# Layer 1 attention on one core: the value products of two steps issued in one block, with four slots for the exponentials

## What is computed

```python
q = jnp.dot(x, Wq).reshape(b, t, H, HD).transpose(0, 2, 1, 3)
kv = jnp.dot(x, Wkv).reshape(b, t, G, 2, HD).transpose(2, 3, 0, 1, 4)
k, v = (kv[:, 0], kv[:, 1])          # each repeated for the 4 heads of its group
scores = jnp.einsum('bhqd,bhkd->bhqk', q, k)
scores = jnp.where(causal[None, None], -jnp.inf, scores)
weights = jax.nn.softmax(scores * (1.0 / HD ** 0.5), axis=-1)
ctx = jnp.einsum('bhqk,bhkd->bhqd', weights, v)
```

## Time and profile before

| | |
|---|---|
| three runs | 1753.5, 1756.12, 1759.4 us; median 1756.12 |
| profiled execution | 1757.35 us, of which the span of the trace is 1755.6 us |
| PE busy over the span | 1650.3 us (94%) |
| DVE, ACT, POOL busy | 1085.6 (62%), 847.8 (48%), 709.1 (40%) |
| stage of layer 1 attention | about 1290 to 1560 us |

### The profile page before, as it was taken

How to read it: one execution, slowest core, us unless ns; L and a number is a source line. 1 busy time by engine, 2 the same in 40 slices (tenths; PEclk the granted TensorE clock), 3 DMA queues, 4 the chain that set the end, 5 groups by cost and what they waited for, 6 DMA issues and landing times. The chain is left out here.

```text
span 1755.6 us, 27326 instructions
## 1 busy us (share of the span) xinstructions
PE 1650.3 (94%) x8874; PEld 1232.9 (70%) x8874; DVE 1085.6 (62%) x2491; ACT 847.8 (48%) x1595; POOL 709.1 (40%) x735
## 2 busy tenths in 40 slices
PE   5899999999988999999999999799999999999998
PEld 5688887788777667766677766577765555568887
DVE  3545657999838677777777776345756777510222
ACT  3456556443326555555555555343135565653321
POOL 1112213444647566665566665385001111322221
PEclk9999999999999999999999999899969999999999
DMA  8522223221110001000001000463622342231111
GB/s 238 167 76 91 88 73 102 56 65 29 54 37 1 19 19 37 19 19 19 19 19 37 19 19 13 127 197 121 174 34 50 73 76 62 51 95 61 48 49 48
DMA packets 110716, 114.16 MB, mean 65 GB/s; under 512 B 39520, under 2 KB 71744, under 8 KB 110592
## 3 DMA queue, kind: packets, MB, share of 16 engines
q1 hardware_dynamic: 108288, 108.40, 22.2%
q10 hardware_dynamic: 2304, 4.20, 0.7%
HBM read 83.97 MB, written 28.44 MB: 64 GB/s over the span
## 5 line engine op out<-in xcount | busy, mean ns | idle before, releaser
L1447 ACT ACTIVATE a_p<-a_sm,a_nmax 128x640 f32<-128x640 f32 (+7 forms) x256 | 198.7, 778 | 142.9 <-DVE a_nmax L1408 141.3
L1490 POOL TENSOR_SCALAR a_p<-a_p,a_rinv 128x640 f32<-128x640 f32 (+7 forms) x256 | 190.6, 748 | 167.8 <-DVE a_rinv L1416 166.4
L1408 DVE CUSTOM_DVE_ANT_0 a_sm<-ps,maskb 128x640 f32<-128x640 f32 (+7 forms) x256 | 192.0, 750 | 100.4 <-PE ps L1352 98.4
L2334 DVE CUSTOM_DVE_ANT_0 ga_sm<-ps,strip 128x640 f32<-128x640 f32 (+1 forms) x224 | 163.3, 755 | 80.4 <-PE ps L2241 78.8
L2354 ACT ACTIVATE ga_pt<-ps 128x1024 f32<-128x1024 f32 (+1 forms) x192 | 148.1, 810 | 114.3 <-PE ps L2264 113.5
L1364 PE MATMUL ps<-ident,a_p 128*128 128x128 f32 x1152 | 172.5, 275 | 12.8 <-DVE a_pt L1423 12.5
L1364 PEld LDWEIGHTS ps<-ident,a_p 128*128 128x128 f32 x1152 | 132.8, 140 | 39.5 <-issue 16.9
L2394 POOL TENSOR_SCALAR_AFFINE_SELECT ga_pt<-ga_pt 128x512 f32<-128x512 f32 x64 | 40.6, 635 | 287.5 <-ACT ga_pt L2354 287.3
L1352 PE MATMUL ps<-kh,lq_qh 128*128 128x512 f32 (+3 forms) x384 | 129.0, 390 | 17.5 <-DVE a_nmax L1408 10.6
L923 DVE SCALAR_TENSOR_TENSOR idx<-ix_r,ix_sgc,idx 128x256 f32<-128x256 f32 (+6 forms) x105 | 90.8, 885 | 76.2 <-ACT ix_r L888 76.2
L1379 PE MATMUL ps<-a_pt,vst 128*64 128x512 f32 (+3 forms) x768 | 135.7, 496 | 1.8 <-DVE a_pt L1423 1.1
(11 more groups left out here) (319 smaller groups left out, 4015.2 us busy)
## 6 DMA issues: line engine op xcount, KB each, us to landing
ctx_d<-a_ctxst SPq DMA_DIRECT2D x16, 512.0 KB, 2.9
idx<-ctx_d SPq DMA_DIRECT2D x32, 256.0 KB, 3.7
idx<-wvo_d SPq DMA_DIRECT2D x32, 256.0 KB, 4.4
ga_qst<-qkd SPq DMA_DIRECT2D x42, 128.0 KB, 4.2
f_wr<-in_L_ffn_w SPq DMA_DIRECT2D x18, 256.0 KB, 2.7
x<-in_L_attn_hidden_states SPq DMA_DIRECT2D x16, 256.0 KB, 4.5
op_wo<-in_L_attn_o_w SPq DMA_DIRECT2D x8, 512.0 KB, 4.4
ix_w<-in_L_attn_idx_wq_w SPq DMA_DIRECT2D x64, 64.0 KB, 1.9
```

Of the source, the lines that this page charges most:

```text
L1408: dve.tensor_tensor_reduce(out=sm[kind][:, 0:w], in0=slots[kind][:, 0:w], in1=maskb[:, MASK_OFF[t]:MASK_OFF[t + 1]], scale=-scale, scalar= ...
L1447: act.activation(p[kind][:, v // 2 % 2, 0:w], sm[kind][:, 0:w], ACT.Exp, bias=nmax[:, v % 4:v % 4 + 1], scale=-1.0, accum_out=rsum[:, v % ...
L1490: pool.tensor_scalar(mine, mine, rinv[:, v % 4:v % 4 + 1], 1.0, ALU.mult, ALU.mult).then_inc(norm_done, 1)
L2334: dve.tensor_tensor_reduce(out=sm[kind][:, 0:w], in0=slots[kind][:, 0:w], in1=strip[:, S - w:], scale=-1.0, scalar=3.0e38, op0=ALU.add, op ...
```

## The change

Two edits in `grouped_attention`. The ring `ga_pt` has four slots, not three, so that ACT's exponential of step n waits for the weigh of step n - 4. And PE issues no `weigh` in even steps; in an odd step (from the third of the whole stage on) it issues two at the place of the one, that of three steps before and that of two steps before.

```diff
-    RING = 3
+    RING = 4
     NB = NB1
     LAG = 2
     LEAD = 3
...
                         if s == NSTEP - LEAD and g + 1 < G1:
                             turn(g + 1)
-                        if g * NSTEP + s >= LAG:
-                            weigh((g * NSTEP + s - LAG) // NSTEP, (g * NSTEP + s - LAG) % NSTEP)
+                        if s % 2 and g * NSTEP + s > LAG:
+                            for n in (g * NSTEP + s - LAG - 1, g * NSTEP + s - LAG):
+                                weigh(n // NSTEP, n % NSTEP)
                         for v in units[two:]:
                             score(later, v)
```

## The result

The change makes the kernel slower. The median of six runs is 1795.6 us (1787.5 to 1796.9) against 1757.8 of before (1753.5 to 1765.3); the ratio is 1.021, 95% interval 1.019 to 1.024. The forecast was 1772, range 1754 to 1782: the direction is right, the size is not: 38 us came where 16 were forecast.

The account below looks back on a forecast made before the run. PE's list (94% busy) and the chain unit, DVE maximum, next unit in the same slot were taken as bounds. Terms 11.3 + 1.5 + 2.2 + 1.0 = 16.0 us gave 1773.4, or 1772 by the median; range 1754 to 1782.

Parts of the forecast that it names:

- the walk: Layer 1's attention, one full group followed by pairs of steps: lateness sums to 2.27 us per group, 16.0 in all; 70%.
- 0, 1: Step 0's weigh was free beside a DVE wait; step 1 takes two weighs, 0.79 us for 0.37: +0.42.
- 2, 3: Step 2 loses a 512 weigh (-1.18) but waits 0.53 for its slot; step 3 gets 0.85 more: +0.20.
- 4, 5: Step 4's 640 waits for the 1024; step 5's block grows by 0.43, partly hidden by its DVE wait: +0.1.
- 6, 7: Largest term: step 6's 512 weigh lay inside a wait; its stream returns in step 7 and DVE falls behind: +0.85.
- 8, 9: Step 8 waits 0.77 for the 896's slot, so some 0.4 is gained; step 9 gets 0.85 more: +0.5.
- 10, 11: Keys p=1 of step 11 wait 0.52 us for ACT's exponentials, against 0.32 saved: +0.2.
- pauses over 1 us in steps 0, 6 and 8: Sign expected on PE before the unit weight loads (L2241), PE's DVE waits rising from some 3 to some 7 us per group.
- Groups 0, 6 and 7: Groups outside the five full ones: 1.5 us for group 0's later steps, 2.2 for group 6, 1.0 for group 7.
- The rival's own price: Clock falls to 0.50 with longer PE pauses: ten us in each of seven groups, 35 us, 1792; 3%.
- The gain side: Joining two weighs saves up to 0.08 + 0.14 + 0.10 = 0.32 us per block in switches and fixed cost.
- The prediction's sum over all 47 blocks: Rival that PE alone counts: 47 switches saved at 0.32 us in all eight groups, 15.0 us, 1742; 15%.

Follow-up runs that it names:

- The fill run: Changed kernel with keys p=1 of even steps in groups 0 to 6 issued twice and 128-column units seven times: 1780.5 us, ratio 1.012 against before.
- the short maximum: DVE's maximum over only the first 128 keys per unit: 1731.6 us in the order of before, 1724.0 changed, 1730.0 with only wide steps' weighs joined.

## Why the prediction was right and wrong

**The waits (the path right, the size somewhat too small).** At full clock one can add the pairs of steps of the changed kernel from keys to keys: steps 0 and 1 from 1450.45 to 1457.09, 6.64 us; 2 and 3, 4.07; 4 and 5, 1423.42 to 1429.81, 6.39; 6 and 7, 1429.81 to 1437.42, 7.61; 8 and 9 in group 0, 1317.31 to 1324.88, 7.57; 10 and 11, 1324.88 to 1328.75, 3.87. In all 36.15 us for 33.49. Against the walk:

| steps | forecast | measured |
|---|---|---|
| 0, 1 | +0.42 | +0.31 |
| 2, 3 | +0.20 | +0.31 |
| 4, 5 | +0.1 | +0.30 |
| 6, 7 | +0.85 | +0.86 |
| 8, 9 | +0.5 | +0.57 |
| 10, 11 | +0.2 | +0.31 |
| group | +2.27 | +2.66 |

The path was the forecast's: free weighs beside DVE's pauses, two streams in the odd step, DVE idle behind them, ACT ahead of step 11. One sign that the prediction named did not come so: it expected pauses over 1 us in steps 0, 6 and 8, and only that of step 6 is (1.26; those of steps 0 and 8 are 0.61). Groups 1 to 5 thus give 13.3 us and not 11.3. Groups 0, 6 and 7 can be read in the same way, pair by pair at full clock: 1.7, 3.3 (its steps 8 to 11 taken from the run with the narrow units filled, where no stretch touches them) and 1.2, for the forecast's 1.5, 2.2 and 1.0. The waits make about 19 of the 38 us, where the walk had 16.

**The clock (wrong).** The step that failed is in the rivals: "the pauses near 1 us leave the clock at 1.00, and the new ones are under 1.5", with 3% for the case, so that the sum had no term for it. The new pauses were as small as said (the longest 1.3 us), and the clock fell all the same. I had judged pauses one by one, by the longest; what changed is that a group has more of them, 6.0 us of idle time for 2.5, in steps 0, 1, 2, 4, 6, 8 and 9. The other 19 us of the 38 are the clock's, for 47.8 us at half of it. They can be read in the profile after, where the same pair of steps, 6 and 7, stands in groups 1, 2 and 3 with 6.8 us at the lower clock, with 3.4, and with none:

```profile
1350.00:1360.76 10.76, 9.34 (x35) 4.54 (x35) 5.65 (x15) 4.19 (x5) 0.00 (x0) 0.68 0.13 39
1390.49:1399.63 9.14, 7.72 (x35) 4.18 (x35) 5.65 (x15) 4.20 (x5) 0.00 (x0) 0.81 0.16 57
1429.81:1437.42 7.61, 6.20 (x36) 3.37 (x35) 5.43 (x15) 4.09 (x5) 0.00 (x0) 1.00 0.19 62
```

Taken so for every pair, against the same pair at full clock, the stretches cost 7.3, 4.3, 1.6, 1.6, 4.4 and 1.1 us in groups 1 to 6, together 20.2. Against that, group 0 came up to 1.00 some 3.6 us earlier than before (0.94 over 1302 to 1306, for the 0.50 of the earlier trace rows), so that group 1 starts 0.3 us late and not 1.7: 1.5 us less. Waits and clock make 19.2 + 20.2 - 1.5 = 37.9 of the 38.0 us. The fill run supports the split from another side, since it has no fall after group 0. From the first transpose of the stage to its last weigh it takes 254.1 us, for 234.5 before and 273.4 after; less six times 0.2 us of filling that leaves 18.4 us for the waits behind that transpose, and 20.5 for the clock. The rival's own price, 35 us for ten us of half clock in each of seven groups, was given in place of the walk; it should have come on top, with a size of its own. That its 1792 lies near the measured time is luck: it has no waits in it, and nearly twice the clock's cost. The range ended at 1782 because the two were never added.

**The gain side (too large).** The 0.32 us per joined block was read in group 7, where a weigh's neighbours are 512 columns wide. The 0.14 of its fixed part is confirmed. The rest depends on the neighbours: with the short maximum the whole saving is 0.25 us in the pair of steps 0 and 1 and 0.03 in that of 4 and 5. The rule of the Trainium skill (TensorEngine Tiling, Key Properties) that a change of tiling mode drains the engine fits the row of group 7, as before; no run here shows the drain by itself. The prediction's sum over all 47 blocks, 15 us and 1742, is not to be had in this order even with nearly all of DVE's waits gone: there the whole change moves a full group by +0.15 us.

**Open.** What exactly brings the clock down: the keys' and the narrow units' filling together keep it up, either alone does not, and shorter pauses before the 640 by themselves changed nothing. The clock can't be held, so its 20 us are read from pairs of steps with and without a stretch, and not from a run in which it alone was changed.

## What to carry to other kernels

When an operation is moved, ask whether it stood in a gap of its engine: there it was free, and at its new place its whole stream counts, which may also starve the engine that made the gap. Price a saved switch between the neighbours it will have, not between those of the row where it is easiest to read. And where a change adds idle time to TensorE, add a term for the granted clock to the sum, even if each pause is short.

## What was not expected of the hardware

The granted clock fell to 0.50 with no pause of PE over 1.3 us in the stage (with the narrow units filled, with none over 0.64), and matmuls 128 columns wide in these pauses (seven for one) did not prevent it (47.8 us at half clock by the trace's record with and without them), while repeating two 512-wide keys matmuls in even steps took it to 27.3 us, and both together to none. A matmul without a use, in a pause, can so make a kernel faster: 1780.5 for 1795.6 us. It did not make up for the change: before it was 1757.8.
